# AdaLN block with routed experts: the gate rows for the expert part are broadcast in two halves, at two places of the load queue

## The reference

```python
mod = (_silu(L0_c) @ L0_wmod).reshape(L0_c.shape[0], 6, 1, -1)
sa, ca, ga, sb, cb, gb = (mod[:, 0], ..., mod[:, 5])       # one row of 256 per sequence
ga, gb = sign * maximum(abs, 0.25)
h = _layernorm(x) * (1 + ca) + sa
x = x + ga * attention(h)
h = _layernorm(x) * (1 + cb) + sb
x = x + gb * ffn(h)
# ffn(h): a shared gelu MLP on all rows, plus, for each sequence and each of 16 experts,
#   the 64 rows with the highest gate score: (gelu(x Wg) * (x Wu)) Wd * score, added to their rows
```

## Time and profile before

| what | value |
|---|---|
| median of 3 runs | 2467.9 us (2467.69, 2467.9, 2471.45) |
| span of the profiled execution, first to last instruction | 2465.3 us |
| median less that span: what lies around it | 2.6 us |
| TensorE / VectorE / ScalarE / GpSimd busy | 96% / 64% / 42% / 47% |
| mean granted TensorE clock, as a share of full speed | 0.987 |
| moved by the load queue (q1) / by GpSimd's queue (q0) | 97.85 MB / 67.14 MB |

### The profile page before, as it was taken

One profiled execution on the slowest core, in us unless ns is written; L12 is line 12 of the kernel. 1 busy time (PEld: TensorE's weight loads), 2 busy tenths in 40 slices (PEclk: granted clock), 3 DMA queues, 4 the chain that ended last, 5 costly groups with the idle time before them and its releaser, 6 DMA issues.

```text
span 2465.3 us, 40995 instructions
## 1 busy us (share of the span) xinstructions
PE 2372.3 (96%) x14388; PEld 2086.3 (85%) x14388; DVE 1567.9 (64%) x3198; ACT 1032.8 (42%) x1912; POOL 1150.4 (47%) x997
## 2 busy tenths in 40 slices
PE   6999999999998999999987999999999999999997
PEld 5888888888887888888876888888888888888886
DVE  6677767778776877788846455555554545555553
ACT  3545545444553545545442333333333333333332
POOL 1233333333332333333352666666666666666664
PEclk9999999999998999999998999999999999999999
DMA  2111111111111111111115444443444444434433
GB/s 90 53 44 59 51 60 60 52 51 57 54 61 44 60 43 60 52 60 60 59 62 90 86 90 82 88 84 66 79 84 87 86 85 88 84 60 86 84 62 43
DMA packets 78506, 167.03 MB, mean 68 GB/s; under 512 B 11744, under 2 KB 46720, under 8 KB 78368
## 3 DMA queue, kind: packets, MB, share of 16 engines
q0 software_dynamic: 49152, 67.14, 16.7%
q1 hardware_dynamic: 29216, 97.85, 11.8%
HBM read 97.71 MB, written 67.24 MB: 67 GB/s over the span
## 4 chain that ended last, share of the span: by engine, by line
PE 84%; DVE 6%; issue 4%; POOL 2%; DMA 1%; ACT 1%; SPq 0%; DVEq 0%; POOLq 0%; ACTq 0%
PE ps L349 26%; PE ps L351 26%; PE ps L350 26%; PE ps L501 2%; DVE stage L856 2%; PE ps L387 1%; DVE bn_stats L758 1%; PE ps L420 1%; DMA stage<-in_wd 1%; DVE x_t L753 1%; PE ps L442 1%; DVE hidden L753 1%; POOL rstd L1144 1%; POOL out L1209 1%; ACT x_t L693 0%
## 5 line engine op out<-in xcount | busy, mean ns | idle before, releaser
L349 PE MATMUL ps<-x_t,weights 128*128 128x512 f32 x1536 | 617.3, 402 | 23.2 <-DVE hidden_f L1111 13.3
L350 PE MATMUL ps<-x_t,weights 128*128 128x512 f32 x1536 | 602.5, 392 | 0.0
L351 PE MATMUL ps<-x_t,weights 128*128 128x512 f32 x1536 | 601.8, 392 | 0.0
L1209 POOL DMA_INDIRECT out<-x_rows,step_token x256 | 418.1, 1633 | 333.9 <-DVE x_rows L1090 275.4
L349 PE MATMUL ps<-weights,hidden 128*128 128x256 f32 x1536 | 435.8, 284 | 8.7 <-POOL hidden L1148 5.6
L351 PE MATMUL ps<-weights,hidden 128*128 128x256 f32 x1536 | 436.1, 284 | 0.0
L350 PE MATMUL ps<-weights,hidden 128*128 128x256 f32 x1536 | 436.0, 284 | 0.0
L1111 DVE TENSOR_TENSOR hidden_f<-gelu,ps 128x512 f32<-128x512 f32 x256 | 175.7, 686 | 379.0 <-ACT gelu L733 348.1
L733 ACT ACTIVATE gelu<-ps 128x512 f32<-128x512 f32 x256 | 152.8, 597 | 535.8 <-PE ps L351 508.4
L349 PEld LDWEIGHTS ps<-x_t,weights 128*128 128x128 f32 x1536 | 290.6, 189 | 83.6 <-DVE hidden_f L1111 13.5
L1148 POOL TENSOR_TENSOR hidden<-hidden_f,hidden 128x512 fp32r<-128x512 f32 x128 | 165.5, 1293 | 408.7 <-ACT hidden L647 408.7
(11 more groups left out here) (174 smaller groups left out, 4436.9 us busy)
## 6 DMA issues: line engine op xcount, KB each, us to landing
x_rows<-in_x SPq DMA_DIRECT2D x32, 512.0 KB, 3.5
pairs<-mod_rows SPq DMA_DIRECT2D x32, 512.0 KB, 4.3
h_rows<-stage SPq DMA_DIRECT2D x32, 512.0 KB, 2.6
out<-y_rows SPq DMA_DIRECT2D x32, 512.0 KB, 2.9
stage<-in_wg SPq DMA_DIRECT2D x16, 512.0 KB, 3.4
stage<-in_wd SPq DMA_DIRECT2D x16, 512.0 KB, 4.4
stage<-in_wu SPq DMA_DIRECT2D x16, 512.0 KB
x_rows<-h_rows,step_token POOLq DMA_INDIRECT x256
```

The lines of the kernel that those rows point to most:

```text
L349: pe.matmul(o, lhs(HI), rhs(HI), start=start, stop=False)
L350: pe.matmul(o, lhs(HI), rhs(LO), start=False, stop=False)
L351: return pe.matmul(o, lhs(LO), rhs(HI), start=False, stop=stop)
L1209: pool.indirect_dma_start(out=out_rows, out_offset=bass.IndirectOffsetOnAxis(ap=ICUR[g][:, t:t + 1], axis=0), in_=X1[:, g % 2, t * D:(t + ...
```

## The change

The two broadcasts of 1 MB are replaced by four of 512 KB: two for slots 0 to 7 in iteration 32, behind the load of the middle third of expert 0, and two for slots 8 to 15 in part B, behind the three weight loads of step 0. VectorE waits for the first two at step 1, as before, and for the last two at step 3.

```diff
                 if at(i, B):
+                    sp.wait_ge(exp_done, T * B)
+                    sp.wait_ge(at_done, T * B)
                     sp.wait_ge(h2t_done, KD * B)
                     sp.wait_ge(h2_stored, 16 * B)
                     sp.dma_start(STAGE[:, WCOLS:2 * WCOLS], w_exp[1][0]).then_inc(w_in, 16)
+                if at(i, B):
+                    gate_pairs(0)
...
+            def gate_pairs(first):
+
+                for half in range(2):
+                    gb = mod_dram.rearrange("(a h) (m d) -> h m a d", h=2, m=NMOD)[half, GB, first:first + B // 4]
+                    sp.dma_start(PAIRS[half * CAP:(half + 1) * CAP, first:first + B // 4, :],
+                                 gb.unsqueeze(0).to_broadcast((CAP, B // 4, D))).then_inc(pairs_in, 16)
+
             phase_a(sp, iteration)
-
-
-            sp.wait_ge(exp_done, T * B)
-            sp.wait_ge(at_done, T * B)
-            sp.wait_ge(y_read, B)
-            for half in range(2):
-                gb = mod_dram.rearrange("(a h) (m d) -> h m a d", h=2, m=NMOD)[half, GB]
-                sp.dma_start(PAIRS[half * CAP:(half + 1) * CAP, :, :],
-                             gb.unsqueeze(0).to_broadcast((CAP, B // 2, D))).then_inc(pairs_in, 16)
...
+                if at(e, 0) and g == 1:
+                    sp.wait_ge(y_read, B)
+                    gate_pairs(B // 4)
...
                 if at(e, 0) and g == 1:
                     dve.wait_ge(pairs_in, 32)
                     dve.wait_ge(y_ready, B)
+                if at(e, 0) and g == 3:
+                    dve.wait_ge(pairs_in, 64)
```

## The result

The changed kernel takes 2455.1 us in the median of 4 runs (2451.57 to 2457.11), the kernel before 2469.68 us beside it (2467.69 to 2472.64): a ratio of 0.9942, 95% interval 0.9930 to 0.9953; the medians are 14.6 us apart. The forecast was 2449.5 us, from 18.4 us saved of 2467.9, and its range ended at 2455.0. Of the 5.6 us between forecast and measurement, 1.8 are the higher median of the kernel before and 3.8 are missing from the saving. In a later comparison the same file took 2451.26 us in 6 runs, the kernel before 2466.92: ratio 0.9933 (0.9919 to 0.9946), 15.7 us apart. So the direction holds, the first median lies just above the range and the second inside it, and the gain is some 3 to 4 us smaller than forecast.

A forecast was written before the change was run, and what follows sets the result against it. TensorE bounds the kernel, idling 13.32 us at the joint because expert 1's weights queue behind the broadcasts' packets. 2467.9 less 18.4 (17.6 from the wait, 0.8 clock) gives 2449.5 us, chance 0.66; 8-in-10 range 2447.0 to 2455.0.

The forecast's parts named there:

- part 1: Expert 1's weights: issued right behind the output store, they land about 1302 to 1303 us, ending ScalarE's wait, margin 5 us.
- The price of a packet: Load queue at 1303 to 1306 us: 0.193 us per packet of about 1 KB, so 24.7 us for 128 per engine.
- part 2: How much reaches the end: ScalarE starts 18.8 us sooner, VectorE gains 17.6, and the shift stays 17.6, less at most 0.6.
- part 3: TensorE at full clock without its 13 us gap: up to 1.7 us more, of which VectorE lets 0.8 count.
- the sum: Whole saving: 17.6 us from the ended wait plus 0.8 us of clock, 18.4 us.
- part 4: First half, about 1266 us: its 1024 packets may delay the first gather; costed at nothing, bounds 0 and 2.3 us.
- Rival A: Late first gather: TensorE's last shared down product slips up to 2.3 us, perhaps some clock; 2450.5 to 2453.5 us, chance 0.20.
- B: Weights still partly late, sharing the engines with the second half: ScalarE gains 10.7 us; 2457.2 us, chance 0.06.
- C: No change, as VectorE or TensorE would have been late anyway: 2467.9 us, chance 0.05.
- D: Slower: the gather of step 2 is starved until beyond the second half; a 25 us stall gives 2474.5 us, chance 0.03.

The follow-up runs named there:

- all behind the weights: Changed kernel with nothing in iteration 32, all four broadcasts behind the weight loads: 2453.86 us, ratio 0.9949; in a second comparison 2454.18 us, 0.9941.
- old order, wide: Kernel before, broadcasts still ahead of the weights, but gate rows first copied to a contiguous place in DRAM: 2454.99 us, ratio 0.9953.
- no broadcast: Kernel before with both broadcasts of the gate rows left out: 2454.12 us, ratio 0.9947.

## Why the prediction was right, and where it was wrong

**What bounds the kernel, and the weights (part 1): right.** Three independent edits that let the weights through, by order, by packet width, or by leaving the broadcasts out, all end ScalarE's wait and save 13 to 17 us in the medians. The price of a packet had some luck in it. 0.193 us holds for the 3 us of the earlier trace rows alone; from 1308 to 1311 us the same queue moved nearly twice as many:

```profile
q1 hardware_dynamic: 494, 0.49, 98.6%
```

That is 3 x 16 x 0.986 / 494 = 0.096 us each, so the 24.7 us for 128 packets came near the measured 26.9 us to landing partly because the slow stretch was the one taken.

**How much reaches the slots' read (part 2) and the clock in step 2 (part 3): right.** 84.84 - 66.24 = 18.6 us where nothing disturbs the joint (66.20 to 66.34 us in five executions of four kernels), 18.4 forecast. VectorE's split follows its top-64 work at once, and the slots' read no longer waits for TensorE. The marks on the way agree too (the split of the weights 44.1 us after the start of the joint, 44.3 forecast), so this is not luck.

**The step that failed is the clock in the sum, together with part 4's "so I cost it at nothing; the bounds are 0 and 2.3 us".** The sum of 18.4 us has the clock only as a gain (0.8 us, part 3) and no term for anything that slows the engines ahead of the weights or behind step 2. Rival A had "a piece of clock" there, up to 1.7 us, only as a follower of the late gather, and with 2450.5 to 2453.5 us it was too small as well. The profiled execution of the changed kernel, laid beside its second one, which lost nothing, shows what stood in its place:

| what | us lost at the joint |
|---|---|
| TensorE's wait for the gather beyond the slack | 0.3 |
| low clock (0.81 and 0.77 over 8 us): the shared down product ends 1.6 us late, less that 0.3 | 1.3 |
| VectorE's scores held beside GpSimd's add: the transposes of the scores 3.3 us late | 1.7 |
| taken up again before the slots' read | -0.4 |
| sum, 69.11 - 66.21 | 2.9 |

Behind the joint, the gap ahead of the transposes for step 3 (1.9 to 2.0 us in every profile) was followed by full clock in the three profiles with the stall. In seven of ten without it the clock fell to 0.72 over 6 us, and the next transposes came 1.6 us later (19.27 against 17.65 us; 1.2 later than the 18.07 of the first profile of before). From the load of the middle third to those next transposes it is 84.84 + 8.59 + 18.07 = 111.50 us before and 69.11 + 8.63 + 19.27 = 97.01 with the change: 14.5 us saved, close to the 14.6 between the medians.

No profile without the stall kept full clock at both places. The five with a clean joint all had the fall in step 3, and the three spared there had it at the joint; two had it at both. So the forecast of 18.4 us with nothing behind it was reached in none of the ten. What decides between the two places isn't explained.

**The late gather itself.** From 1273 to 1276 us only the load queue moves packets (first row). From 1279 to 1282 us the gather moves as well (second row); at 1279 us some 800 of the 1024 small packets are through:

```profile
q1 hardware_dynamic: 231, 0.24, 59.4%
```

```profile
q0 software_dynamic: 74, 0.20, 18.8%
```

It starts some 10 us after the load of the middle third; the prediction had 10.6, but by another rule, the end of the first broadcast with its 512 packets. The Trainium skill's round robin, cited in part 4 (DMA: Bandwidth & Descriptors, "Queues, rings and completion order"), would have had the gather there before 1280 us on the scale of the kernel before, with no wait. All four executions with the early half have one, so here the measurement decides against it. But the wait is within the slack in three of the four. Whether it makes a fall of the clock more likely isn't shown: the clock fell at the joint in three of the four executions with a late gather, there already in the first 4 of the 12 us of the table, and in four of the nine without one.

**The range** allowed 1.5 us above rival A for the spread of executions, from three runs that spanned 3.8 us. The runs of before in one later comparison spanned 13.5 us (2460.74 to 2474.23), and the profiled ones alone reach the middle third's load between 1262.80 and 1268.88 us. That allowance was too small.

**What stays open.** The two profiles of the changed kernel give 84.84 or 86.15 less 66.21 to 69.11, some 17.8 us in the mean at the joint, and 1.2 to 1.6 of it is given back. Its two medians give 14.6 and 15.7. What is left over is within the intervals. Whether the edit itself is 1 us better or worse than having everything behind the weights can't be told from these runs: 0.9942 and 0.9933 against 0.9949 and 0.9941.

Rivals B, C and D are out: the weights came in time although the second half followed at once, the wait disappeared, and the gather of step 2 caused none.

## What to carry to other kernels

When one stage waits for a load, look in its queue for what stands in front and isn't needed yet, and count its packets rather than its bytes. Swapping the order cost nothing here, since the displaced transfer had slack. Moving it earlier instead put it in front of something else, the first gather. Removing a stall also removes a cushion: disturbances that the stall used to hide, here of clock and of engines meeting, start to count, so a forecast of the full stall is an upper end, not a middle. And several profiled executions are needed before a loss of 3 us is laid at a kernel's door.

## What the runs showed that I had not expected

**VectorE held by a GpSimd add.** In five executions VectorE's small SBUF-to-SBUF instruction (scores or their copy) started within 0.5 us of GpSimd's 2.38 us add or during it, and took 2.57, 3.11, 2.62, 2.66 and 2.18 us instead of 0.22 or 0.43. It ended 0.1 to 0.3 us after the add each time. Where the scores were over before, they took 0.22 to 0.23 us. VectorE's copy from PSUM ran beside the same add undisturbed (1.08 us in the first profile of the kernel before). So the engines don't meet at semaphores alone, as the description of the chip had it. The Trainium skill (SBUF — State Buffer, "Who interferes with whom") describes a port pair shared by the two engines and held for a whole instruction by the one that issues first; these rows agree on the holding. On the order they don't: in four of the five VectorE's recorded start is the earlier one, by 0.10 to 0.45 us, and it still ended after the add. The recorded starts may not be the moments of issue, so this stays open.

**A queue silent behind another.** GpSimd's gather of step 2 moved nothing for some 12, 9 and 7 us after its issue where weights and broadcasts of 1 KB packets were in the load queue (before, changed, all behind the weights), for some 7 us with packets of 16 KB (old order, wide), and for some 2 us with the weights alone (no broadcast). So the silence isn't a matter of small packets only. It ended before the load queue was empty, and the two then ran side by side: before, 192 packets of the gather went beside the second broadcast. What ends it isn't explained.

**The clock can fall after a wait that it survives in another execution.** TensorE's wait of 2.86 us for GpSimd left the clock at full in five profiles. In four others with the same wait it fell, in the second one of the kernel before to 0.51 over 4 us.
